# Second attention of a four-stage transformer kernel: softmax weights turned by DMA in 16-bit pairs

## The reference

```python
q, k, v = ((x @ W.T).reshape(B, T, H, Dh) for W in (Wq, Wk, Wv))
q, k = _apply_rope(q, cos, sin), _apply_rope(k, cos, sin)
scores = jnp.einsum('bthd,bshd->bhts', q, k) * scale
scores = jnp.where(causal[None, None], scores, -jnp.inf)
attn = jax.nn.softmax(scores, axis=-1)
y = jnp.einsum('bhts,bshd->bthd', attn, v).reshape(B, T, H * Dh)
return y / 3.0 @ Wo.T
```

## Time and profile before

| what | value |
|---|---|
| median of three runs (lowest, highest) | 2009.21 us (2007.48, 2012.58) |
| profiled execution: span from the first to the last instruction; no other time of it is given | 2012.9 us |
| busy in that span: PE, DVE, ACT, POOL | 96%, 71%, 65%, 47% |
| second attention, from its first projection to its last product | 474 to 1912 us |

### The profile page before, as it was taken

The page is one execution under the profiler, slowest core; times in us unless marked ns, Lnnn a source line. Parts: engine busy times, 40 slices in busy tenths (PEclk is TensorE's granted clock), DMA queues, the critical chain, the costliest instruction groups (busy, mean ns, idle before and its releaser), DMA issues.

```text
span 2012.9 us, 40239 instructions
## 1 busy us (share of the span) xinstructions
PE 1931.8 (96%) x13726; PEld 1757.7 (87%) x13726; DVE 1433.8 (71%) x3587; ACT 1315.8 (65%) x3367; POOL 939.7 (47%) x961
## 2 busy tenths in 40 slices
PE   6888989998999999999999999999999999999899
PEld 5678857787999999999999999999999999998888
DVE  8378653756878778687877868787777878777753
ACT  4346533444778677777867777787777778776652
POOL 2641126534554636545463554545365554536242
PEclk9999999999999999999999999999999999999999
DMA  8750177500000000000000000000000000000000
GB/s 292 195 100 2 48 241 172 121 1 9 9 9 6 10 7 4 7 9 9 7 9 7 4 7 9 9 7 9 7 4 7 9 9 7 9 6 2 22 27 32
DMA packets 58600, 73.44 MB, mean 36 GB/s; under 512 B 9760, under 2 KB 45216, under 8 KB 58272
## 3 DMA queue, kind: packets, MB, share of 16 engines
q1 hardware_dynamic: 48032, 58.03, 9.0%
q0 software_dynamic: 10368, 12.85, 3.9%
HBM read 51.06 MB, written 19.80 MB: 35 GB/s over the span
## 4 chain that ended last, share of the span: by engine, by line
PE 60%; DVE 11%; ACT 9%; POOL 7%; issue 7%; DMA 0%; ACTq 0%; another core or an unknown queue 0%; POOLq 0%; DVEq 0%
PE phase_scores L1271 16%; PE phase_ring L1329 9%; PE phase_y L167 5%; PE phase_y L166 5%; PE phase_y L165 5%; PE phase_ring L165 4%; PE phase_ring L167 4%; PE phase_ring L166 4%; ACT phase_p L1303 4%; DVE phase_scores L1282 2%; POOL phase_rot L2511 2%; POOL phase_straight L2509 2%; PE phase_up_ps L165 2%; PE phase_up_ps L167 1%; PE phase_up_ps L166 1%
## 5 line engine op out<-in xcount | busy, mean ns | idle before, releaser
L1303 ACT ACTIVATE phase_p<-phase_scores,phase_bias 128x512 f32<-128x512 f32 (+3 forms) x680 | 417.5, 628 | 117.4 <-DVE phase_bias L1291 116.8
L1349 DVE TENSOR_TENSOR phase_pt_lo<-phase_ring,phase_pt_hi 128x512 fp32r<-128x512 f32 (+3 forms) x680 | 390.7, 603 | 90.4 <-ACT phase_pt_hi L1344 86.5
L1344 ACT ACTIVATE phase_pt_hi<-phase_ring 128x512 fp32r<-128x512 f32 (+3 forms) x680 | 343.1, 536 | 105.1 <-PE phase_ring L1329 101.7
L1329 PE MATMUL phase_ring<-sb_ident,phase_p 128*128 128x128 f32 x2312 | 340.5, 273 | 13.0 <-ACT phase_p L1303 7.4
L165 PE MATMUL phase_y<-phase_pt_hi,phase_v_hi 128*128 128x256 f32 (+1 forms) x1152 | 341.2, 296 | 6.7 <-DVE phase_y_lo L2485 6.7
L167 PE MATMUL phase_y<-phase_pt_hi,phase_v_lo 128*128 128x256 f32 (+1 forms) x1152 | 321.2, 279 | 0.0
L166 PE MATMUL phase_y<-phase_pt_lo,phase_v_hi 128*128 128x256 f32 (+1 forms) x1152 | 321.2, 279 | 0.0
L1329 PEld LDWEIGHTS phase_ring<-sb_ident,phase_p 128*128 128x128 f32 x2312 | 271.6, 140 | 54.3 <-ACT phase_p L1303 17.7
L1284 DVE TENSOR_REDUCE phase_peaks<-phase_scores 128x1 f32<-128x512 f32 (+1 forms) x408 | 265.8, 666 | 46.0 <-PE phase_scores L1271 43.6
L2509 POOL TENSOR_TENSOR phase_straight<-phase_rot,late_rope 64x512 f32<-64x512 f32 x128 | 164.0, 1281 | 275.2 <-ACT phase_rot L2378 275.1
L2526 POOL TENSOR_TENSOR sb_x<-sb_x,phase_part 128x512 f32<-128x512 f32 x128 | 165.1, 1290 | 252.8 <-ACT phase_part L2413 246.4
(11 more groups left out here) (292 smaller groups left out, 4836.3 us busy)
## 6 DMA issues: line engine op xcount, KB each, us to landing
y_rows<-phase_zero SPq DMA_DIRECT2D x16, 512.0 KB, 7.6
phase_e_up<-expert_up SPq DMA_DIRECT2D x16, 352.0 KB
phase_e_dn<-expert_down SPq DMA_DIRECT2D x16, 256.0 KB
xn_rows<-phase_ln_xn SPq DMA_DIRECT2D x8, 512.0 KB, 2.9
sb_x<-y_rows POOLq DMA_DIRECT2D x8, 512.0 KB, 6.6
late_raw_qk<-qk SPq DMA_DIRECT2D x16, 256.0 KB, 2.7
phase_logits_t<-expert_up SPq DMA_DIRECT2D x8, 352.0 KB
phase_ln_xn<-expert_up SPq DMA_DIRECT2D x8, 352.0 KB
```

Of the source, the lines that this page charges most:

```text
L1303: act.activation(self.p[:, at:at + width], self.scores[:, at:at + width], ACT.Exp, bias=self.bias[:, t % 2:t % 2 + 1], accum_out=self.sums ...
L1329: done = pe.transpose(bank[:, j * P:(j + 1) * P], self.p[:, (4 * place + j) * P:(4 * place + j + 1) * P], self.core.ident[:])
L1344: act.activation(hi, value, ACT.Copy).then_inc(*self.t_hi.one)
L1349: dve.tensor_tensor(lo, value, as_f32(hi), ALU.subtract).then_inc(*self.t_lo.one)
```

## The change

In attention1 alone, PE no longer turns the weights. A turn step now does this: ACT writes `hi` = p x 2^14 rounded to a 16-bit float, from `p` in SBUF to one of four split rooms (`split`); DVE writes `lo` = p x 2^14 - hi in 16 bits beside it, both inputs in SBUF; SP issues one transposing DMA for the tile and chunk, which turns up to four blocks of both halves (up to 256 KB) into `pt`, now with rooms for three pairs of tiles. SP walks the whole list of steps for this, and issues the loads of weights at their places in it. pv waits for the DMAs of its two tiles. The values are also kept in 16-bit pairs, scaled by a power of a bound from the sum of the squares of Wv (new steps bound and share, eight of each; seven new ACT squares, one more in the stage before), on two sides, by turns; Wo takes the scales back. Several semaphores are shared under new names. The core of the diff:

```diff
@@ class Softmax @@
             if old := self.old_chunk[h, t, c]:
-                act.wait_ge(*self.turned[old])
+                act.wait_ge(*self.p_read(old))
@@ class Attention1 @@
-    RING = ("project", "values", "turn", "out", "flip", "next_flip")
+    RING = ("project", "values", "bound", "out", "flip", "next_flip")
+    SPLIT_ROOMS, PAIR_ROOMS, SHARE = 4, 3, 2.0 ** 14
+    def turned_rooms(self, sb):
+        self.split = sb("split", [P, self.SPLIT_ROOMS, 4, 2, P], F16)
+        self.turned_rest = sb.rest()
+        self.pt = sb("pt", [P, self.PAIR_ROOMS, NT, 2, 2 * P], F16)
...
-        self.v_hi, self.v_lo = (sb(n, [P, NT, 2 * DH], F32R) for n in ("v_hi", "v_lo"))
+        self.v_hi, self.v_lo = (sb(n, [P, 2, NT, 2 * DH], F16) for n in ("v_hi", "v_lo"))
...
+    def p_read(self, key):
+        return self.t_lo[key]
+    def old_pair(self, h, t, b):
+        if (old := self.before((h, t // 2), self.PAIR_ROOMS)) is None:
+            return None
+        return self.weighed[(*old, min(self.blocks(t, b)[-1], 2 * old[1] + 1))]
+    def act_split(self, act, key):
+        hi, lo, value = self.split_views(key)
+        act.wait_ge(*self.p_done[key])
+        if (n := self.turn_at[key]) >= self.SPLIT_ROOMS:
+            act.wait_ge(*self.laid[n % self.SPLIT_ROOMS][self.turns[n - self.SPLIT_ROOMS]])
+        act.activation(hi, value, ACT.Copy, scale=self.SHARE).then_inc(*self.t_hi.one)
+    def dve_split(self, dve, key):
+        hi, lo, value = self.split_views(key)
+        dve.wait_ge(*self.t_hi[key])
+        dve.scalar_tensor_tensor(lo, value, self.SHARE, hi, ALU.mult, ALU.subtract).then_inc(*self.t_lo.one)
+    def sp_turn(self, sp, key):
+        h, t, b = key
+        keys, r = self.blocks(t, b), self.turn_at[key] % self.SPLIT_ROOMS
+        sp.wait_ge(*self.t_lo[key])
+        if old := self.old_pair(*key):
+            sp.wait_ge(*old)
+        out = self.pt[:, self.pair_room(h, t // 2), keys.start:keys.stop, :, (t % 2) * P:(t % 2 + 1) * P]
+        sp.dma_start_transpose(out.rearrange("p j s q -> p (j s) q"),
+                               self.split[:, r, 0:len(keys)].rearrange("p j s k -> p (j s k)")).then_inc(*self.laid[r].one)
+    def pe_wait_laid(self, pe, h, g, j):
+        for t in (2 * g, 2 * g + 1):
+            if j <= t and (j == 0 or self.chunk(t, j) != self.chunk(t, j - 1)):
+                key = h, t, self.chunk(t, j)
+                pe.wait_ge(*self.laid[self.turn_at[key] % self.SPLIT_ROOMS][key])
@@ def sp @@
         for step in self.order:
-            if step[0] == "load_qk":
+            if step[0] == "turn":
+                if step[1:] == (NH - 1, NT // 4, 0):
+                    self.sp_next_weights(sp)
+                self.sp_turn(sp, step[1:])
+            elif step[0] == "load_qk":
@@ def pe @@
-            elif what == "turn":
-                self.pe_turn(pe, key)
...
-                if j % 4 == 0:
-                    pe.wait_ge(*self.t_lo[h, 2 * g + 1, j // 4])
+                self.pe_wait_laid(pe, h, g, j)
...
-                products(pe, self.y[:, q], [self.v_hi[:, j, v]], [self.v_lo[:, j, v]],
-                         [(self.pt_hi[buf][:, j, q], self.pt_lo[buf][:, j, q])], first=j == 0, last=j == 2 * g + 1).then_inc(*self.weighed.one)
+                products(pe, self.y[:, q], [self.v_hi[:, side, j, v]], [self.v_lo[:, side, j, v]],
+                         [(self.pt[:, room, j, 0, q], self.pt[:, room, j, 1, q])], first=j == 0, last=j == 2 * g + 1).then_inc(*self.weighed.one)
@@ def act, def act_weights @@
             elif what == "turn":
-                self.act_turn(act, key, self.old_pt(*key))
+                self.act_split(act, key)
...
+        if name == "wv":
+            if n >= 2:
+                act.wait_ge(*self.bounded[n - 2,])
+            act.activation(self.core.squares[:], raw[:].rearrange("p k h -> p (k h)"), ACT.Square,
+                           accum_out=self.core.power[:, n % 2:n % 2 + 1]).then_inc(*self.squared.one)
@@ def dve @@
-                self.dve_turn(dve, key)
+                self.dve_split(dve, key)
```

More of the change, by code:

```diff
@@ L477, in __init__ @@
             s.plan(one)
-        self.expert_in = [core.loads(f"expert_in{s}") for s in range(self.SLOTS)]
+        self.expert_in = [core.loads(f"filled{s}") for s in range(self.SLOTS)]
         for n, key in enumerate(experts):
@@ L2154, in __init__ @@
             s.plan(ends)
+        turns = of("turn")
+        self.turns, self.turn_at = turns, {key: n for n, key in enumerate(turns)}
+        self.laid = [core.loads(f"filled{r}") for r in range(self.SPLIT_ROOMS)]
+        for n, key in enumerate(turns):
+            self.laid[n % self.SPLIT_ROOMS].plan([key])
+        self.filled = core.flag("attn_ones")
+        self.filled.plan([tag])
+        self.squared, self.bounded, self.bound_kept = sig("wv_squared"), sig("wv_bound"), sig("wv_kept")
+        self.v_scaled, self.spread_done, self.shared = sig("v_scale"), sig("spread"), sig("wo_scale")
+        self.squared.plan(of("bound")[1:])
+        for s in (self.bounded, self.bound_kept, self.v_scaled):
+            s.plan(of("bound"))
+        for s in (self.spread_done, self.shared):
+            s.plan(of("share"))
         self.follower = None
@@ L2203, in plan_order @@
                     elif letter == "w" and h % 2:
-                        steps = [("load_wv", h // 2 + 1)]
+                        steps = [("load_wv", h // 2 + 1), ("bound", h // 2 + 1)]
+                    elif letter == "u" and h % 2:
+                        steps = [("share", h // 2 + 1)]
                     elif letter == "l":
@@ L2210, in plan_order @@
                         steps = [next(late)]
-                    order += [step for step in steps if 0 <= step[1] < (NH // 2 if step[0] in ("values", "load_wv") else NH)]
+                    order += [step for step in steps if 0 <= step[1] < (NH // 2 if step[0] in ("values", "load_wv", "bound", "share") else NH)]
         order.append(("out", NH - 1, G - 2))
@@ L2223, in ring_read @@
             return norm.lo[(norm.tag, *step[1:])]
[L2224 to L2231, removed]
+        return {"bound": self.bound_kept, "project": self.rotated, "values": self.v_lo_done, "out": self.parted}[step[0]][step[1:]]
@@ L2312, in pe @@
                 self.pe_score(pe, key, pairs)
-            elif what == "turn":
-                self.pe_turn(pe, key)
+            elif what == "bound":
+                n, = key
+                pe.wait_ge(*(self.squared[key] if n else self.prior.next_squared[self.tag]))
+                if n == 0:
+                    pe.wait_ge(*self.filled[self.tag])
+                self.pe_ring_wait(pe, step)
+                pe.matmul(self.ring_bank(step)[:, 0:1], self.ones[:], core.power[:, n % 2:n % 2 + 1], start=True, stop=True).then_inc(*self.bounded.one)
             elif what == "values":
@@ L2492, in pool @@
             what, key = step[0], step[1:]
-            if what == "stats":
+            if what == "bound":
+                n, = key
+                pool.wait_ge(*idle)
+                pool.wait_ge(*self.bound_kept[key])
+                if n >= 2:
+                    pool.wait_ge(*self.v_lo_done[n - 2, G - 1])
+                    pool.wait_ge(*self.shared[n - 2,])
+                pool.tensor_tensor(self.v_scale[:, n % 2:n % 2 + 1], self.bound[:, n % 2:n % 2 + 1], self.core.half[:, 0:1], ALU.pow).then_inc(*self.v_scaled.one)
+                idle = self.v_scaled[key]
+            elif what == "stats":
                 pool.wait_ge(*idle)
```

90 lines of the change are left out of this document (67 added, 23 removed).

## The result

The changed kernel takes 2355.8 us (median of 4 runs, 2353.8 to 2357.3) against 2009.3 us before on the same chip: a ratio of 1.172, 95% interval 1.170 to 1.174. The forecast was 2068 us: slower, as said, but by 346 us and not by 59.

The account below looks back on a forecast made before the run. TensorE bounds the kernel before; VectorE was to bound the changed second attention: 1093 work + 175 GpSimd waits + 128 loads + 101 idle = 1497 us, 59 over 1438, giving 2068 us; own range 1955 to 2171, range of all 1890 to 2445.

Parts of the forecast that it names:

- The two costs: Second attention: VectorE's splits waiting for GpSimd, 175 us, and ScalarE and VectorE standing behind weight loads, 128 us.
- The formula for a random meeting: VectorE's splits: each meets a GpSimd operation at random, 0.48 x 0.568 = 0.274 us a split, 175 us in all.
- Rival B: Splits fall between GpSimd's operations, so the 175 us vanish: stage 1322 us, kernel 1893 us; chance 0.28.
- The loads' term: SP's queue: ScalarE waits for weight loads issued behind transposing DMAs, 38 times, 128 us; bounds nothing and some 170 us.
- The upper bound that I gave: SP's queue: waits behind loads cost some 170 us if a transposing DMA's issue takes a microsecond more.
- the sum itself: Second attention, VectorE as bound: 1093 + 175 + 128 + 101 = 1497 us, 59 more than 1438.
- The forecast's own range: Whole kernel: 1955 us with loads hidden, to 2171 us with 0.59 us lost per split.
- Rival C: Transposing DMAs bound the second attention, 0.43 us for each of 4352 blocks: 1871 us, kernel 2442 us; chance 0.22.
- Costed at nothing: Transposing DMAs' 142.6 MB keep the queue busy 446 to 870 us beside a stage of 1500, adding no time.
- Rival D: No change: waits behind loads and for GpSimd fall half together, stage 1438 us, kernel 2009 us; chance 0.08.
- TensorE at most 1175 us: Second attention: TensorE's work after losing 215 us of transposes and 48 us through 16-bit products, from 1438 us.
- Small things: Ring, values' sides, bound, scale and share steps, and the last DMA wait: 10 us at most for the tiny steps, 0 taken.

Follow-up runs that it names:

- loads in turn: Kernel before, with SP waiting at each turn's place for VectorE's second half, no transposing DMAs, so weight loads keep their place in the order: 2176.2 us, ratio 1.078.
- both costs taken off: Changed kernel with weight loads issued early and VectorE's split reading zeros from PSUM as one input, ring of two banks: 2029.5 us, ratio 1.006.
- idle products: Changed kernel with weight loads issued early, plus 2048 identity products on TensorE that nothing waits for: ratio 1.118.

## Why the prediction was right and wrong

**The two costs were the right ones.** VectorE's splits are stretched by GpSimd: forecast 175 us, measured 571.0 - 367.5 = 203.5, mean 0.92 us in the page's row against 0.88 foreseen. The formula for a random meeting was 14% low; with the share that GpSimd was really busy (782 of 1780 us, 0.44 and not 0.48) it gives 160 us, 21% low. The rule of the Trainium skill (SBUF - State Buffer, Who interferes with whom) is borne out from both sides: with the other input from SBUF the old operation took 581.2 us, with one input from PSUM the new one 367.9. Rival B falls: the order does not keep the two apart.

**The loads' term was too small.** Forecast 128 us by 3.0 to 3.9 us for each of 38; the waits are 212 us, 7.4, 5.2 and 4.0 us for qk, wv and wo, and removing them brought 203. The step "the issue of the last transposing DMA (0.43 us, like a plain issue; its lower bound)" failed: it is 1.23 us in the median, two stand ahead of each load of qk, and ScalarE also stands while VectorE finishes the splits that these two wait for (1.6 us in the timeline above). The upper bound that I gave, some 170 us for an issue a microsecond longer, counted one issue and no such splits.

**The step that failed for the total is the sum itself.** It read: "DVE is the bound: 1093 of work, 175 of waits for POOL, 128 behind the loads, and of its present idle time the 101 us [...]; its other waits [...] I let go since ACT has room." VectorE was idle for 345 us of the old stage (1438 - 1093); the sum keeps 101 of them and puts the other 244 at nothing, so that the new costs fill them. The only reason given was ScalarE's room. The runs show little of that. With the loads out of the way VectorE still idles for 278 of 1576 us, where the sum leaves it 101. The stage before lost 119 us to 203 us more work on VectorE, so four tenths of it were covered; it lost 158 us to loads in turn and 292 to both; and it gave back 30 us when 1536 transposes left it. A sum that fits starts at the old stage, not at VectorE's busy time: 1438 + 10 (16-bit form) + 131 (splits beside GpSimd) + 203 (loads) = 1782 us, and 1780 were measured. It is made afterwards, from terms that the runs measured, and shows that they add; it forecast nothing. With my own sizes it would have been 1438 + 175 x 0.6 + 128 = 1671 us, 2242 us of time, if one takes the 0.6 that a run showed. The waits that I let go did not shrink: VectorE's for the first half of the weights went from 84.0 us to 164.6, that for y from 101.1 to 135.0, ScalarE's for the bias from 97.8 to 294.9. A part of the first two is standing behind loads: with loads early they are 67.4 and 75.5, the third still 284.6. Why VectorE's idle time can't be filled, wait by wait, stays open.

**Two bounds were added wrongly.** The forecast's own range reads 1955 to 2171 us. By its own terms it is 2068 - 128 = 1940 at the low end, and with 1322 + 378 = 1700 us of stage, 262 over 1438, it is 2271 at the high end. The measured 2356 lies outside both.

**Rival C had the price near and the cause wrong.** SP waits for VectorE in the stage and not the other way round; TensorE's waits for a landing are 18.2 + 4.9 us, where 100 were to show C, and ScalarE's for split rooms 20.9. The landing of 3.1 us was foreseen to the digit, and a whole turn of up to four pairs of blocks is issued in 1.23 us. The Trainium skill (VectorE: DVE Perf Modes, The three transpose paths) has 1309 ns for one 128x128 block; taken block after block that does not hold here, where a DMA of eight blocks is issued in 1.23 us and lands in some 3.1. Costed at nothing was right for the queue's rate: the run with both costs taken off stands at 1.006, the same kernel turned by TensorE at 1.005. As the near price came from other causes, it was luck. **Rival D** falls too: the two costs add (0.101 + 0.065 of 0.172) and don't fall half together.

**TensorE at most 1175 us** came out as 1325.4 busy. The clock has a part in it (0.87 of full speed in the stage), and so has the measure: 1175 was added up from distances between starts, and the busy time has the modelled ends of products in it. With the clock at 0.96 it is still 1228.5; how the rest divides is not shown. Small things at 0 to 10 us: 10 us measured. The bound step's wait in TensorE's queue (43.7 us, 7 times, for ScalarE's squares, which wait for the load) is inside the loads' term: with loads early it is 5.8 us.

## What to carry to other kernels

When the engines of a stage hand work around in a written order, test for a second limit before counting on the first engine's relief: take the work off it, leave the rest, and see what moves. New costs on the other engines went on top of the old stage here, at full price where all of them waited (a load in the queue), at some 0.6 where one had more to do. And before a queue gets work that waits, look at what else lives in it: here a dozen lines that issue the loads some tiles ahead were worth 203 us, though even so the change doesn't pay. Of the versions with the whole computation none beat the kernel before: 2019.8 us turned by TensorE in 16 bits, 2153.8 us by DMA with early loads.

## What the runs showed of the hardware

- A transposing DMA from SBUF to SBUF of 128 rows by 256 to 1024 16-bit values: 1.23 us of the issuing engine in the median (1.17 for 256 values, 1.23 for 1024, so hardly a matter of size), 3.1 us to the landing. With 86 GB/s over the stage (after) the engines stood 44 us in all for these landings, with 106 GB/s (both costs off) 80 us.
- TensorE's granted clock, the mean over the stage, fell where TensorE stood more: 1.00 in the stage before (busy 1413 of 1438 us), 0.96 with both costs off (1229 of 1458), 0.92 with early loads (1269 of 1576), 0.87 after (1325 of 1780), so between the levels of 2.4 and 1.2 GHz; with the idle products put in it was 0.99 (1604 of 1677). With TensorE's work as before and only the loads in turn it was 0.95 (1472 of 1602). That run is busier than the one at 0.96, so the busy share alone doesn't order them. Single products got longer too. This group of the kernel after has 437 ns at most; the same group has 284 at most in the run where TensorE turned the 16-bit weights, at a clock of 1.00:

```profile
L166 PE MATMUL phase_y<-phase_pt,phase_v_hi x1152: 218/273/437, 504.1 to 2252.8; 128*128 128x256 f16 x192
```

  What this cost by itself was not separated: the run that raised the clock also added TensorE work.
- GpSimd loses as well where VectorE reads two SBUF inputs: 59.7 us in the stage after (722.2 to 781.9), 68.1 in the kernel before with that one edit.
